# A fused attention and mixture-of-experts kernel: in the first nine tiles of its middle the normalised input is turned and split one step earlier, and kv's copy stands ahead of feats on VectorE

## What is computed

```python
xn = _ln(q_x, ln1_w, ln1_b)
q, k, v = (xn @ wq + bq), (xn @ wk + bk), (xn @ wv + bv)      # 16 heads of 16
fq, fk = elu(q) + 1, elu(k) + 1
kv   = einsum('bhnd,bhne->bnde', fk, v)                        # per token, summed over heads
qkv  = einsum('bhnd,bnde->bhne', fq, kv)
qk   = einsum('bhnd,bnd->bhn', fq, fk.sum(axis=1))
attn = (qkv / (qk[..., None] + 1e-6)) @ wo + bo
x = q_x + attn
h = gelu(_ln(x, ln2_w, ln2_b) @ fc_w + fc_b)
return x + (h @ proj_w + proj_b)
```

## Time and profile before

| | |
|---|---|
| Median of 3 runs | 729.17 us (728.81 to 731.09) |
| The profiled execution's own time | 728.32 us |
| Its span, first to last instruction | 726.6 us |
| Busy in the span: TensorE, VectorE, ScalarE, GpSimd | 670.2, 480.7, 420.1, 326.5 us |
| Mean granted TensorE clock | 0.972 |
| Chain that ended last, by engine | TensorE 75%, VectorE 8%, issue 6%, ScalarE 4% |

### The profile page before, as it was taken

The page is one execution under the profiler, slowest core; times in us unless marked ns, Lnnn a source line. Parts: engine busy times, 40 slices in busy tenths (PEclk is TensorE's granted clock), DMA queues, the critical chain, the costliest instruction groups (busy, mean ns, idle before and its releaser), DMA issues.

```text
span 726.6 us, 17451 instructions
## 1 busy us (share of the span) xinstructions
PE 670.2 (92%) x6214; PEld 567.2 (78%) x6214; DVE 480.7 (66%) x1332; ACT 420.1 (58%) x841; POOL 326.5 (45%) x493
## 2 busy tenths in 40 slices
PE   7689999997778999999999999999999876999994
PEld 5449999974566788888888888888888663999994
DVE  7846756425688766767868768677676565767751
ACT  5755556512335767676767676767754642766660
POOL 5252563122233453545573755746538464253312
PEclk9769999999999999999999999999999996999998
DMA  8479788404756444544655555455434344477720
GB/s 266 152 251 307 225 271 279 139 29 119 103 98 105 91 66 90 95 88 66 101 94 105 94 91 117 67 109 89 87 70 122 105 138 103 150 216 217 221 93 29
DMA packets 287103, 95.56 MB, mean 132 GB/s; under 512 B 213988, under 2 KB 284736, under 8 KB 287018
## 3 DMA queue, kind: packets, MB, share of 16 engines
q1 hardware_dynamic: 272298, 85.48, 48.2%
q0 software_dynamic: 3840, 8.32, 3.7%
q10 hardware_dynamic: 10880, 0.66, 1.0%
HBM read 65.09 MB, written 29.40 MB: 130 GB/s over the span
## 4 chain that ended last, share of the span: by engine, by line
PE 75%; DVE 8%; issue 6%; ACT 4%; POOL 3%; DMA 1%; ACTq 1%; SPq 0%; POOLq 0%; DVEq 0%
PE bank L1728 67%; PE bank L1737 7%; POOL hids L788 1%; ACT feats L992 1%; POOL xb_rows L683 1%; ACT feats L994 1%; DMA xb_rows<-late_rows,xb_token 1%; ACT hids L1031 1%; DVE kv_ L1672 1%; DMA x_all<-in_L_attn_q_x_dram 1%; POOL table L671 1%; DVE ra_mark L1471 0%; ACT ots L1056 0%; ACT kvt_ L1018 0%; DVE sth L1680 0%
## 5 line engine op out<-in xcount | busy, mean ns | idle before, releaser
L1728 PE MATMUL bank<-down_w,hids 128*128 128x256 f32 x768 | 105.9, 286 | 1.9 <-POOL hids L788 1.6
L1728 PE MATMUL bank<-hnts,up_w 128*128 128x512 f32 x384 | 104.4, 407 | 0.0
L788 POOL TENSOR_TENSOR hids<-hid,hids 128x512 fp32r<-128x512 f32 x64 | 83.1, 1299 | 41.1 <-ACT hids L1031 40.7
L1728 PEld LDWEIGHTS bank<-down_w,hids 128*128 128x128 f32 x768 | 95.7, 188 | 6.1 <-POOL hids L788 3.3
L1728 PE MATMUL bank<-qkv_w,xnts 128*128 128x256 f32 (+1 forms) x384 | 76.3, 346 | 5.7 <-DVE xnts L1582 4.8
L1728 PEld LDWEIGHTS bank<-hnts,up_w 128*128 128x128 f32 x384 | 67.5, 189 | 11.5
L1728 PEld LDWEIGHTS bank<-qkv_w,xnts 128*128 128x128 f32 x384 | 60.6, 189 | 18.2 <-DVE xnts L1582 7.5
L1028 ACT ACTIVATE hid<-bank,cols 128x512 f32<-128x512 f32 x64 | 44.1, 688 | 45.9 <-PE bank L1728 45.6
L779 POOL TENSOR_SCALAR sth<-sth 128x1 f32<-128x1 f32 x32 | 7.2, 225 | 124.3 <-DVE sth L1594 124.2
L1728 PE MATMUL bank<-a_w,xa_h 128*128 128x256 f32 x256 | 60.2, 379 | 0.0
L1728 PE MATMUL bank<-xa_xt,a_w 128*128 128x256 f32 x384 | 55.1, 294 | 1.4 <-DVE xa_xt L1320 1.4
(11 more groups left out here) (272 smaller groups left out, 1545.4 us busy)
## 6 DMA issues: line engine op xcount, KB each, us to landing
qkv_rows<-feats SPq DMA_DIRECT2D x32, 384.0 KB, 3.0
a_raw<-in_L_ffn_w_dram SPq DMA_DIRECT2D x32, 256.0 KB, 4.2
a_w<-in_L_ffn_w_dram SPq DMA_DIRECT2D x32, 256.0 KB, 4.2
b_raw<-in_L_ffn_w_dram SPq DMA_DIRECT2D x32, 256.0 KB, 3.1
b_w<-in_L_ffn_w_dram SPq DMA_DIRECT2D x32, 256.0 KB, 3.0
mid_rows<-x_all SPq DMA_DIRECT2D x8, 512.0 KB, 2.9
x<-mid_rows SPq DMA_DIRECT2D x32, 128.0 KB, 2.3
values<-qkv_rows SPq DMA_DIRECT2D x32, 128.0 KB, 2.9
```

What stands on the lines that cost most here:

```text
L788: pool.tensor_tensor(hids[1][u % 3][:], hid[u % 2][:], f32(hids[0][u % 3][:]), ALU.subtract).then_inc(s_hidl, 1)
L1728: return pe.matmul(dst, left, right, start=start, stop=stop, skip_group_check=True)
```

## The change

For tiles 0 to 8 the turn of `zn` on TensorE, the cast on ScalarE and the low half on VectorE are done in step n + 1, the step that makes `zn`, and no longer in step n + 2. A helper tells for each step which of the two it is. For tiles 9 to 31 all three stay in step n + 2; step 10 turns no tile. In the early steps the turn stands on TensorE behind `qkv` of the tile before and ahead of `turn_kv`, the cast on ScalarE behind the three instructions of `qkv` and ahead of the cast of `hn`, and the low half on VectorE behind `feats` and `kv` and ahead of `xo`. Also, in steps before `UP_FROM` (10) VectorE copies `kv` ahead of completing `feats`, no longer behind it.

```diff
--- before.py
+++ after.py
@@ -326,6 +326,11 @@
 
         def at(s, k):
             return s - k if 0 <= s - k < NT else None
+
+        def zn_turned_at(s, early):
+
+            n = s - 1 if early else s - 2
+            return n if 0 <= n < NT and (n < UP_FROM - 1) == early else None
 
         def group_at(s, first):
             g, t = divmod(s - first, GROUP)
@@ -1035,7 +1040,7 @@
             act.wait_ge(s_wlow, len(chunks))
             act.wait_ge(s_folded, 2)
             for s in range(MID_STEPS):
-                if at(s, 2) is not None:
+                if zn_turned_at(s, False) is not None:
                     turn_zn(s - 2)
                 if s == 4:
                     help_queries(0)
@@ -1073,6 +1078,8 @@
                     help_keys(0)
                 for n in turned_at(s, 0):
                     features(n, bank[B_TURN])
+                if zn_turned_at(s, True) is not None:
+                    turn_zn(s - 1)
                 if at(s, 6) is not None:
                     turn_h(s - 6)
                 if at(s, 3) is not None and 1 <= s - 3 < HELPED:
@@ -1618,7 +1625,7 @@
                     dve.tensor_tensor(cols[:, C_FCB:C_FCB + KM], bank[B_DOWN][:, 0:KM], cols[:, C_FCB:C_FCB + KM],
                                       ALU.add).then_inc(s_fcb, 1)
 
-                if n2 is not None:
+                if zn_turned_at(s, False) is not None:
                     low_zn(n2)
                 if routed(s, 2) is not None and routed(s, 2) < NG - 2:
                     read_counts(routed(s, 2), bank[B_KV])
@@ -1660,16 +1667,23 @@
                     dve.wait_ge(s_zn, n1 + 2)
                     dve.scalar_tensor_tensor(out=x1[n1 % 8][:], in0=x1[n1 % 8][:], scalar=st[:, 10:11], in1=pb_row[:],
                                              op0=ALU.subtract, op1=ALU.add).then_inc(s_rest, 1)
+                if n4 is not None and s < UP_FROM:
+                    dve.wait_ge(s_kvturn, n4 + 1)
+                    if n4 >= 1:
+                        dve.wait_ge(s_st2, n4)
+                    dve.tensor_copy(kv[:], bank[B_KV][:].rearrange("p (i c) -> p i c", i=4)).then_inc(s_kv, 1)
                 if n2 is not None:
                     dve.wait_ge(s_soft, 2 * (n2 + 1))
                     soft = feats[n2 % 2][:, 0:2 * D]
                     dve.scalar_tensor_tensor(out=soft, in0=bank[B_QK][:], scalar=0.0, in1=soft,
                                              op0=ALU.max, op1=ALU.add).then_inc(s_feat, 1)
-                if n4 is not None:
+                if n4 is not None and s >= UP_FROM:
                     dve.wait_ge(s_kvturn, n4 + 1)
                     if n4 >= 1:
                         dve.wait_ge(s_st2, n4)
                     dve.tensor_copy(kv[:], bank[B_KV][:].rearrange("p (i c) -> p i c", i=4)).then_inc(s_kv, 1)
+                if zn_turned_at(s, True) is not None:
+                    low_zn(n1)
                 if n5 is not None:
                     n = n5
                     dve.wait_ge(s_wo, n + 1)
@@ -2078,7 +2092,7 @@
             for s in range(MID_STEPS):
                 g_up, j_up = divmod(s - 10, GROUP)
                 g_down, j_down = divmod(s - 11, GROUP)
-                n = at(s, 2)
+                n = zn_turned_at(s, False)
                 if n is not None:
                     dst = bank[B_TURN]
                     pe.wait_ge(s_zn, n + 2)
@@ -2109,6 +2123,16 @@
                 if at(s, 2) is not None and s != 4:
                     qkv(s - 2, v_free)
                     v_free = (s_val, s - 1)
+                n = zn_turned_at(s, True)
+                if n is not None:
+                    dst = bank[B_TURN]
+                    pe.wait_ge(s_zn, n + 2)
+                    if turn_free:
+                        pe.wait_ge(*turn_free)
+                    for k in range(KD):
+                        last = turn(dst[:, k * P:(k + 1) * P], zn[:, k * P:(k + 1) * P])
+                    last.then_inc(s_znt, 1)
+                    turn_free = (s_xnl, n + 1)
                 if 0 <= g_down < NG:
                     down_mid(g_down, 2 * j_down + 1)
                 if at(s, 4) is not None:
```

## The result

The changed kernel takes **731.12 us** (median of 20 runs, 729.97 to 732.96), the kernel before 729.18 us (20 runs on the same chip, 728.39 to 731.09). The two medians differ by 1.94 us. The ratio, estimated from all these runs, is 1.0024 with a 95% interval of 1.0016 to 1.0032, which is +1.75 us (+1.2 to +2.3). That is slower, and clear of zero, but by less than the 0.3% taken here as the limit, which the interval's upper end just passes. The forecast was 730.2 us, a shift of +1.1.

The account below looks back on a forecast made before the run. TensorE fills the middle from 240 us; before it, the ramp's steps are bound by VectorE's ordered queue and its waits. Terms -0.2 + 0.8 + 1.0 - 0.5 = +1.1 us gave a median of 730.2 us, range 728.0 to 732.3.

Parts of the forecast that it names:

- A: Likeliest case, the ramp as computed: +1.1 us, range -0.3 to +2.2 (729 to 731.3 us), chance 0.66.
- Steps 1 to 4: Early ramp: tile 1's low half no longer stands behind the next tile's statistics, so qkv starts earlier: -0.2 us.
- Step 5: Ramp: with kv first, feats and its store come later, delaying ScalarE's key issues and kv_t's copy: +0.8 us.
- Steps 6 to 9: Ramp: the wait for ScalarE goes, the low half and a kv wait come; 0.26 us a step, +1.0 us.
- Step 10: End of ramp: first up product spared a turn (0.2), gelu directly behind its product (0.3): -0.5 us.
- The cover by `xr`: Steps 6 to 9: GpSimd's xr holds den anyway, hiding a new 0.28 us VectorE wait, costed at nothing.
- `den` is short: Sign of being wrong, in steps 6 to 9: den was forecast to stay 0.5 us or longer.
- Rival C: Steps 6 to 9: product with kv too late for its cover; +3.9 us, or +2.5 in milder form; chance 0.14.
- 2.68 after the store: Step 5: ScalarE's key issues were taken to begin 2.68 us after SyncE's store of feats, as before.
- Rival B: Steps 5 to 9: earlier qkv carries the steps, the 0.43 us wait goes; -2.85 us in all, 726.3; chance 0.12.
- Rival D: Ramp: TensorE's clock falls to 1.2 GHz in a step, making it 2 to 5 us longer; 732 to 735; chance 0.04.

Follow-up runs that it names:

- the second trace of after: The changed kernel, unchanged, executed and profiled once more: 730.50 us.
- e1: The changed kernel with feats ahead of kv's copy in all steps, so only the early turn, cast and low half remain: 0.9999 of the kernel before.
- e9: The changed kernel with kv_t turned ahead of zn on TensorE, kv still first: 1.0000 of the kernel before.
- e2: The changed kernel with every tile turned as late as in the kernel before, so only kv ahead of feats remains: 1.0017 of the kernel before.
- e3: The changed kernel with feats ahead of kv's copy again in steps up to 4: 1.0012 of the kernel before.
- e7: The changed kernel with the early turn only from tile 5 on and feats first everywhere: 0.9987 of the kernel before.
- e8: The changed kernel with the early turn only from tile 5 on and kv first in steps 6 to 9: 1.0014 of the kernel before.
- e6: The changed kernel with ScalarE's issues of tile 2's keys in step 5 moved behind its copy of kv_t: 1.0021 of the kernel before.
- e4: The changed kernel with six more idle products on TensorE in step 4, ahead of kv_t's turn: 1.0019 of the kernel before.
- e5: e1 with ScalarE's issues of tile 2's keys in step 5 moved behind its copy of kv_t: 0.9990 of the kernel before.

## Why the prediction was right

It said +1.1 us and "no difference"; +1.75 (+1.2 to +2.3) came, so the time lies in the upper part of A's span, and the 1.1 just below the interval. The mechanism of A is what the runs show. By its steps, with the second trace of after, which has full clock:

| Term | Forecast | Measured |
|---|---|---|
| Steps 1 to 4 | -0.2 | +0.15 |
| Step 5 | +0.8 | +1.18 |
| Steps 6 to 9 | +1.0 | +0.65 |
| Step 10 | -0.5 | -0.36 |
| Sum | +1.1 | +1.62 |

No term but the last is within 0.3 of its forecast. The early steps and step 5 came out dearer by 0.73 together, steps 6 to 9 cheaper by 0.35, so the sum is nearer than its parts, and that much is luck.

**Steps 6 to 9** were walked nearly to the instruction. From t = 0 at 209.49: `zn` turned 2.91 (2.98 forecast), `kvt_` turned 3.18 (3.23), `kv` 3.82 (3.87) with a wait of 0.38 (0.38), `feats` 4.42 without a wait (4.47), low half 5.02 (5.07), `xo` 5.35 (5.43), `hn` turned 5.58 (5.61), product with `kv` 5.92 (5.92), transposition 7.07 (7.04), reciprocal 8.18 (8.27), end 9.26 (9.36). The spacings sum to 0.10 too much on the way, against a term that is itself only 0.16. A difference of two long sums is worth no more than its spacings. The steps took 9.24 to 9.31, just below the 9.3 to 9.4 said. qkv starts 0.93 us earlier in the step than before (209.44, t = -0.05, against t = 0.88), not 0.6.

**The cover by `xr` held.** The transposition is 1.72 us behind `xo`, against 1.33 before, and the reciprocal is 2.83 behind it, against 2.84. The 0.39 vanished in `den`: both end with `xr`. What `den` takes when `xr` is not running is seen in step 4 of the kernel before:

```profile
187.75 0.17 DVE L1571 TENSOR_SCALAR den<-att_ 128x16 f32<-128x16 f32 x1
```

It is 0.17 or 0.18 us in steps 4, 5 and 10 of all thirteen traces, where `xr` is not running when it starts. In steps 6 to 9, where it is, `den` ends 0.02 to 0.04 us after `xr`. The Trainium skill ("SBUF — State Buffer", section "Who interferes with whom") states that whichever of VectorE and GpSimd issues first gets the shared port pair for its whole instruction, and that the other is blocked. The rows agree with it: 0.32 us for an instruction that comes 0.43 into `xr`'s 0.73, and 0.74 for one that comes 0.03 into it. One sign that I had named for being wrong did come: "`den` is short". It was 0.32 where I had written 0.5 or longer. That sign was badly worked out: by my own walk `den` came at 7.78 and `xr` let go at 8.20, which leaves 0.42. The cover that the sign stood for held all the same. Rival C did not come; it needed a transposition later than 7.46.

**Step 5** is the term that was mis-sized most, by 0.38. I had the right chain (`kv` waits for TensorE, `feats` and its store come behind, ScalarE's keys wait for the store, `kvt_` waits for ScalarE). The store went out at t = 21.09 and 21.38, 1.2 and 1.5 later than before, where I had 0.9. What failed too was "2.68 after the store": the time from store to key issues was 2.44 and 3.22 in the two traces of after, and 2.5 to 4.5 in the experiments that leave the issues in place. The issues began at t = 23.82 and 24.31, where I had 23.5. I had also not seen that the early turn alone moves this store: in e1, with `feats` first, it left at 20.30 instead of 19.89, because SyncE reached it later. The loads of tile 1's keys, which stand ahead of it in SyncE's queue, began at 17.20 instead of 16.64.

**Steps 1 to 4** did not give the 0.2. The second `qkv` did start 0.27 earlier (t = 8.41 against 8.68), but VectorE came to its `feats` at 11.66, against 11.67: the gain ended in VectorE's queue. And `feats` of tile 0 was 0.26 later than before (7.34 against 7.08). I had followed the engine that profits and not the one that has to take the result.

**Step 10** gave 0.36, not 0.5. The gelu gained 0.26 behind its product's start (0.3 forecast); that the turn no longer stands ahead of the product gave 0.12 (it stands 2.34 ahead of the aggregate that ends step 9, against 2.22), not 0.2.

**Rival B** would have needed `kv` never to wait. e1 and e9 show how much of it was there: 0.31 a step, 1.24 in four, plus step 10, less what step 5 costs. **Rival D**, the clock, did come, but in a place where I had not looked: in steps 4 and 5 (in steps 6 to 9 only once, in e9's trace). It is in some executions only, and in the profiled one it makes up at most about 0.4 of the 0.71 between 2.33 and 1.62.

## What to carry to other kernels

When one edit makes a result ready earlier, ask which of two neighbouring instructions is then the late one before fixing their order: here, in steps 6 to 9, the exchange of `kv` and `feats` was worth nothing alone and cost 0.47 us a step on top of an edit that by itself gained 0.31. An engine that waits for a store to land in order to issue loads had better not have a critical copy behind it; that wait varied by 2 us from trace to trace, and in e1 it held the copy by 2.2. And a change that pays in the steady steps of a ramp should begin only where the ramp is steady.

## What the runs showed that I had not expected

- **The same store took 2.4 to 4.5 us until ScalarE, which waits for it, issued the next keys.** It is 384 KB, tile 2's features, and sits among 16 KB loads of queries and keys: 2.68 us twice in the kernel before, 2.44 and 3.22 in after, 4.45 in e1, 4.33 in e2, 2.68 in e3, 3.93 in e4, 2.70, 2.71 and 2.50 in e7, e8 and e9. Later stores were not always the slower ones. In the eight traces that turn early from tile 0 on, it landed within 2.7 us in the five where tile 1's store had left at t = 13.55 or later, and took 3.2 to 4.5 in the three where that was at 13.44 or earlier. But the kernel before had 13.37 and 13.15 there, and 2.68. Why it varies stays open.
- **TensorE's clock fell to half (0.50, 1.2 GHz) in steps 4 and 5 in four of thirteen traces**: after, e3, e6 and e9, where it fell in step 9 as well. It was full there in both of before and in e4, the one with fillers. In after, TensorE had waited 1.88 us for ScalarE at 185.60 and 0.78 us for VectorE at 187.05 just before; but the second trace of after waited 1.57 us and e5's 1.85, and both kept their clock. e1 and e3 have the same code up to the end of step 4 and waited 1.60 and 1.65 us there; e3's clock fell within step 4 (four turns of `kvt_` took 0.97 us, in e1 0.66), e1's did not. All four that fell turn early from tile 0; none of the five that turn the first tiles late did (before twice, e2, e7, e8). That the early turn is what makes it possible was not tested. The 14 idle products ahead of the middle were slow too in seven traces (4.73 to 4.87 us, otherwise 3.18), e5 and after's second among them, which had full clock in steps 4 and 5. What decides it was not found.
- **`den`'s length says nothing of its work.** 0.74 us, 0.32 us and, with `xr` out of the way, 0.17 us for the same 128 by 16 elements: where the two overlap it ends when GpSimd's `xr` does. A reader who sees a tiny VectorE instruction of such a length does well to look at what GpSimd has running.
